# Turns of four tiles: the first 128 channels in two banks of 256 columns, copied by ScalarE and VectorE, in place of one bank copied by ScalarE

## The reference

```
def layer_0(x):
    h = layernorm(x) * (1 + ca) + sa
    x = x + ga * causal_attention(h)        # 16 heads of 64, keys and values through a latent of 128
    h = layernorm(x) * (1 + cb) + sb
    return x + gb * (gelu((h @ U1) @ V1 + b1) @ U2 @ V2 + b2)

def layer_1(x):
    h = layernorm(x) * (1 + ca) + sa
    # performer attention with two layer norms of its own: phi(q) . cumsum(phi(k) v) / (phi(q) . cumsum phi(k)),
    # then gelu(y @ w1 + b1) @ w2 + b2
    x = x + ga * performer_block(h)
    h = layernorm(x) * (1 + cb) + sb
    return x + gb * slot_experts(h)          # each of 64 slots picks the best token of a group of 16
```

## Time and profile before

| | |
|---|---|
| median of 3 runs | 1764.78 us (1763.83 to 1767.97) |
| the profiled execution's own time | 1762.62 us |
| its span, first to last instruction | 1761.3 us |
| PE busy | 1695.6 us, 96% |
| DVE busy | 1249.5 us, 71% |
| POOL busy | 867.9 us, 49% |
| ACT busy | 853.4 us, 48% |

### The profile page before, as it was taken

How to read it: one execution, slowest core, us unless ns; L and a number is a source line. 1 busy time by engine, 2 the same in 40 slices (tenths; PEclk the granted TensorE clock), 3 DMA queues, 4 the chain that set the end, 5 groups by cost and what they waited for, 6 DMA issues and landing times.

```text
span 1761.3 us, 41351 instructions
## 1 busy us (share of the span) xinstructions
PE 1695.6 (96%) x16646; PEld 1158.9 (66%) x16646; DVE 1249.5 (71%) x2734; ACT 853.4 (48%) x1872; POOL 867.9 (49%) x1123
## 2 busy tenths in 40 slices
PE   8999999999999999999999999999999999999998
PEld 5566675668566677567856667656685666766667
DVE  5988947626799985753679987675467988676445
ACT  4666624233577753322457674432245676443233
POOL 2788842221188883241128888314113888740420
PEclk9999999999999999999999999999999999999999
DMA  6566570321266664050136665305013665620500
GB/s 187 129 147 149 138 218 34 58 40 38 63 151 141 142 144 151 1 88 10 38 83 150 148 145 136 131 2 97 0 44 94 145 151 139 155 102 2 96 1 26
DMA packets 124653, 172.34 MB, mean 98 GB/s; under 512 B 33744, under 2 KB 90544, under 8 KB 123440
## 3 DMA queue, kind: packets, MB, share of 16 engines
q1 hardware_dynamic: 106272, 162.36, 37.9%
q10 hardware_dynamic: 18192, 7.35, 1.8%
HBM read 79.93 MB, written 4.77 MB: 48 GB/s over the span
## 4 chain that ended last, share of the span: by engine, by line
PE 63%; DVE 14%; POOL 7%; ACT 6%; SPq 4%; issue 4%; DMA 2%; ACTq 0%; POOLq 0%; DVEq 0%
PE scores L467 13%; PE bank L688 8%; PE scores L668 7%; POOL placed L877 5%; PE bank L467 4%; SPq L1024 4%; DVE prob L811 4%; ACT prob L929 3%; PE bank L715 3%; PE scores L1804 2%; PE scores L1714 2%; PE bank L725 2%; DMA placed<-prob 2%; PE bank L719 2%; PE scores L1776 2%
## 5 line engine op out<-in xcount | busy, mean ns | idle before, releaser
L877 POOL COPY placed<-prob 32x768 f32<-32x768 f32 x448 | 368.8, 823 | 210.4 <-DVE prob L811 179.6
L298 POOL TENSOR_TENSOR rstd<-rstd,minus_half 128x2 f32<-128x2 f32 x96 | 69.9, 729 | 537.3 <-DVE rstd L297 535.2
L688 PEld LDWEIGHTS bank<-placed,v_t 128*64 128x64 f32 x4608 | 250.5, 137 | 74.6 <-issue 72.9
L688 PE MATMUL bank<-placed,v_t 128*64 128x128 f32 x4608 | 272.5, 274 | 10.9 <-DMA placed<-prob 7.2
L668 PE MATMUL scores<-k_t,q_t 64*128 64x512 f32 (+3 forms) x1536 | 274.0, 496 | 1.3 <-DVE neg_max L804 1.2
L811 DVE STREAM_TRANSPOSE prob<-prob 128x1536 f32<-128x1536 f32 x128 | 222.6, 1764 | 44.9 <-ACT prob L929 44.7
L804 DVE CUSTOM_DVE_ANT_0 mod_rows<-scores,hx 128x128 f32<-128x128 f32 (+7 forms) x256 | 190.7, 745 | 21.1 <-PE scores L668 21.1
L668 PEld LDWEIGHTS scores<-k_t,q_t 64*128 64x128 f32 x1536 | 130.1, 187 | 113.2 <-issue 91.5
L877 POOL COPY placed<-hx 32x768 f32<-32x768 f32 x224 | 184.6, 824 | 32.5 <-DVE hx L811 15.5
L929 ACT ACTIVATE prob<-mod_rows,neg_max 128x128 f32<-128x128 f32 (+2 forms) x192 | 137.6, 717 | 117.9 <-DVE neg_max L804 117.8
L804 DVE CUSTOM_DVE_ANT_0 x<-scores,hx 128x128 f32<-128x128 f32 (+7 forms) x256 | 192.7, 753 | 0.0
(11 more groups left out here) (245 smaller groups left out, 3198.8 us busy)
## 6 DMA issues: line engine op xcount, KB each, us to landing
placed<-prob SPq DMA_DIRECT2D x576, 96.0 KB, 2.6
f<-in_L_ffn_f SPq DMA_DIRECT2D x16, 2048.0 KB, 13.7
placed<-hx SPq DMA_DIRECT2D x288, 96.0 KB, 2.2
inverse_wide<-inverse_scratch SPq DMA_DIRECT2D x64, 256.0 KB, 4.2
mod_rows<-mod_scratch SPq DMA_DIRECT2D x32, 128.0 KB, 5.0
out<-x SPq DMA_DIRECT2D x16, 256.0 KB, 2.2
w_ring<-in_L_attn_w_q ACTq DMA_DIRECT2D x24, 128.0 KB, 4.2
w_ring<-in_L_attn_w_kv_up ACTq DMA_DIRECT2D x48, 64.0 KB, 2.9
```

The costliest lines, as they stand in the source:

```text
L298: step = pool.do(lambda e, ts=ts: nc.gpsimd.tensor_tensor(rstd[:, ts], rstd[:, ts], minus_half[:, ts], op=ALU.pow), var, filled)
L688: last = nc.tensor.matmul(out_bank[rows_, at_:at_ + P], v_t[pair % 2][:, j, rows_], placed[m % 2][:, :, head, first_block(m, i) + j, :], s ...
L877: nc.gpsimd.tensor_copy(placed[m % 2][target * GROUP:(target + 1) * GROUP, source, :, :, :], prob[m % 3][source * GROUP:(source + 1) * GRO ...
```

## The change

Only `turn` changes, and `Lane.do`, which now also takes a list of steps in `after`. For a turn of four tiles the group c=0 is no longer one bank. A new function `first_half` takes a bank, writes the transposes of two tiles into its first 256 columns and copies these: the first two tiles by ScalarE (`near`), the other two, from a second bank, by VectorE. Both copies together are the first element of `copies`, so the c=0 product waits for both. The group c=1 stays as it is, one bank of 512 columns and one copy by ScalarE. A turn thus takes three banks of the rotation and not two, and each step after it that takes a bank gets another one than before. Turns of two tiles stay as they are. SyncE's and GpSimd's lists have the same steps in the same order, and PE's too, but for the banks that its transposes and products use.

```diff
     def do(self, emit, *after):
-        step = Step(self, emit, [a for a in after if a is not None])
+        flat = [a for one in after for a in (one if isinstance(one, list) else [one])]
+        step = Step(self, emit, [a for a in flat if a is not None])
...
             copies, tiles = [], list(tiles or tiles_of(half))
-            for c in range(C):
+            def first_half(near, tiles_, ready_):
+                i, ps, reader = banks.take()
+                for n, (t, r) in enumerate(zip(tiles_, ready_)):
+                    done = pe.do(lambda e, n=n, t=t: nc.tensor.transpose(ps[:, n * P:(n + 1) * P], src[:, t, 0:P], ident[:, :]),
+                                 r, reader)
+                ps_, o = ps[:, 0:2 * P], dst[:, 0, tiles_[0] * P:(tiles_[-1] + 1) * P]
+                if near and scale is None:
+                    copy = act.do(lambda e: nc.scalar.copy(o, ps_), done, after)
+                elif near:
+                    copy = act.do(lambda e: nc.scalar.activation(o, ps_, ACT.Identity, bias=bias[:, 0:1], scale=scale[:, 0:1]),
+                                  done, after)
+                elif scale is None:
+                    copy = dve.do(lambda e: nc.vector.tensor_copy(o, ps_), done, after)
+                else:
+                    copy = dve.do(lambda e: nc.vector.tensor_scalar(o, ps_, scale[:, 0:1], bias[:, 0:1], op0=ALU.mult,
+                                                                    op1=ALU.add), done, after)
+                banks.read_by(i, copy)
+                return copy
+
+            halved = len(tiles) == TH
+            if halved:
+                copies.append([first_half(near, tiles[k:k + 2], list(ready)[k:k + 2]) for k, near in ((0, True), (2, False))])
+            for c in range(1 if halved else 0, C):
                 i, ps, reader = banks.take()
```

## The result

The changed kernel takes 1789.49 us (median of 4 runs, 1787.65 to 1795.09), the kernel before 1764.85 us (1763.83 to 1767.97). The ratio is 1.0142, with a 95% interval of 1.0116 to 1.0168: slower by 25 us. In a later session the two were run side by side again: 1789.42 against 1762.80 us, ratio 1.0147 (1.0128 to 1.0167). The profiled execution of the changed kernel took 1788.78 us for a span of 1787.5.

What follows compares the result with a forecast made beforehand. The kernel was taken as bound by TensorE, busy 96% of the span. Four batches +14.4, start +3.8 and boundaries +1.2 give +19.4 us on 1764.8, so 1784; 8 in 10 from 1774 to 1796.

Steps and rivals of the forecast that it cites:

- the second rival: PE's clock falls in the new waits, 1.7 us each; at four or eight places 1791 or 1798 us; chance 0.19.
- the waits alone: Main forecast: PE waits for copies queued on DVE and for rotated banks, 1784 us (1779 to 1789); chance 0.60.
- The late turns: Per batch, copy behind other DVE work: feed_turn(0) +0.31, attention_turn(0) +0.61, attention_turn(1) +1.50, attention_sum(1) +1.54 us.
- the start: Program start: first product +3.29 us behind norm steps on DVE; with the rotation's wait at pair 0's queries about +3.8.
- the three boundaries: Batch ends: next queries wait for residual additions reading their banks, +0.6; with shorter ACT copies +0.4 each, 1.2 in all.
- contention and halving theories: From the experiments: copies from neighbouring banks slow each other, 1780 or more; two short copies cost as such, 1785 to 1790.
- the third rival: Part of the delay is taken up again in PE's next waits for DVE: 1778 or 1773 us; chance 0.13.
- From the first product to the first queries: Program start, from 12.45 to pair 0's queries at 19.38: +0.46 us foretold.
- The turns of feed and attention: Per batch, PE's product waits for DVE's copy: feed_turn(0) +0.31, attention_turn(0) +0.61, attention_turn(1) +1.50 us.
- mlp_turn(0): MLP turn where DVE arrives about when the bank is full; product starts sooner, -0.30 us per batch.
- The gap at 59.40: Stretch from 59.40 to 61.40 before the change: PE worked 0.30 of 2.00 us, yet its clock didn't fall.
- the first rival: Two copies run side by side at turns on PE's path, 7 us less, 1758; faster by over 0.3%: chance 0.03.

Runs made afterwards that it cites:

- the filled kernel: Changed kernel plus identity-matrix transposes, results unread, on TensorE ahead of the product in its longest waits; 1786.92 us beside 1789.42 for the changed kernel.

## Why the prediction was right, and where it was short

The forecast was 1784, the measured time 1789.5. That lies inside the range for 8 in 10 (1774 to 1796), but just outside the 1779 to 1789 that had the chance of 0.60, and nearer to the 1791 of the second rival. The case that I held to be the likeliest, the waits alone, is not the one that came.

*The mechanism held.* Each new copy started when VectorE's list had come to it. The late turns, the start and the three boundaries are those named, and each of the late turns lost within 0.07 us of its term. The run with the copies further up in the list took 23 of the 25 us away without moving any work off VectorE, the one with both halves on ScalarE 21. The contention and halving theories had no part in it. The late turns' delays were not taken up again: between the steps of the table TensorE keeps its distance to the kernel before, and the third rival is out.

*The sum was 2 us short in its own terms*, 19.4 against 21.3. Three terms were mis-sized. From the first product to the first queries it was 1.24 and not 0.46, because the half-clock stretch at the start, which I had taken to begin later and to be as long as before, began sooner (11.19) and took in the transposes of the second half and a part of its product as well (clock 0.50 up to 21.4, the last row shown of the start). In the other profile of the changed kernel, where it ended at 18.8, this step was +0.29. The turns of feed and attention lost 0.06 or 0.07 more than foretold, since I gave 0.04 us from the end of a copy to the product, as after ScalarE; after VectorE it is 0.15 (297.77 + 0.54 to 298.46). For the same reason mlp_turn(0) gained 0.17 and not 0.30. The start makes 0.7 of the 1.9 us, mlp_turn(0) 0.5, the late turns the rest.

*The clock was a term, not a rival.* I had treated the falls as another case, with a chance of 0.19 and a time of 1791 or 1798. They came on top of the forecast's sum: the clock was 0.993 to 0.995 in every run of the changed kernel, its two profiles have three and four such stretches behind new waits, and each costs the 1.7 us that was worked out from L467 at either clock. For the profiled execution 1762.6 + 21.3 + 5 gives 1789, and it took 1788.8; that this fits to 0.2 us is in part luck, as 1.1 us made up on the way and 0.8 us lost at the end nearly cancel. For the medians the clock's part is not known that well: the filled kernel, at a clock of 0.999, is only 2.5 us lower. The measured time lies in the range because the range took in this rival. The gap at 59.40, where the clock had not fallen, was the wrong comfort: it was one instance, and the change makes eight waits of 1.8 to 2.0 us and four of 1.1, behind each of which the clock may fall. The Trainium skill (TensorE: Matmul & The Clock Gate, on the HAM clock gate) has idle stretches take the clock away, and on this the fillers agree with it: with TensorE busy in the waits, no stretch at half clock was left between the start and the end of the program in two profiles.

*The gain that the change is meant for is real but small.* Where VectorE is free a turn gets 0.05 to 0.17 us shorter, not 0.3. Two halves side by side save part of a copy's duration, but the product starts only 0.15 us after the VectorE half. At the turns where VectorE is free it gave 1.8 us. With the best that was seen, 0.17 at five turns of a batch and 0.25 at three prologues, it would be some 4 us (an estimate), so the first rival's 7 were not there even with VectorE free.

## What to carry to other kernels

Splitting a copy between two engines pays only if the second engine gets to it in time; what it has in its list ahead of the new step is the price, and it is read in the trace at each place, not from the engine's share of busy time (VectorE was idle for 29% of the span here). When the list order is written by hand, look whether the step can be put further up, and whose bank the steps that it overtakes are reading. A new wait of one to two us on a nearly full TensorE should be priced with a chance of a stretch at half clock, here 1.7 us each in the profiles. And where banks are handed out in rotation, a taken bank more or less moves every later reader: look at the places where the newest reader and the next writer meet, here 0.65 us at a boundary and 1.0 at an MLP.

## What the runs showed of the hardware

- From the end of a VectorE copy to the start of the product waiting for it 0.15 us went by (298.31 to 298.46, 347.94 to 348.08, 254.54 to 254.69, and so at every such place of the changed kernel but the first, which has 0.10), from the end of a ScalarE copy 0.04 (12.41 to 12.45, where the chain of the kernel before has a piece of 0.04 between the copy and the product).
- The clock fell behind waits of 1.0 us (1769.81), 1.1 us (717.77) and 2.0 us (1178.14). It did so at some of the like places and not at others, and at different ones in the two profiles of the changed kernel; the mean clocks of six runs of one kernel lay between 0.990 and 0.997. With fillers it was 0.999 in all eight runs, at no cost to the products behind them.
